# Between two attentions: where GpSimd adds the second bias, and VectorE's order of maxima and rows

## The chip, the cores and the metric

The kernel runs on one core of a Trainium2 chip. The metric is device time in microseconds (us) of one execution, as a median of runs. The five engines each follow a program of their own, in order, and meet only at semaphores: TensorE (PE) multiplies, VectorE (DVE) and ScalarE (ACT) read PE's results, GpSimd (POOL) works on what lies in on-chip memory, and SyncE (SP) issues nearly all transfers.

## The reference

One decoder layer over 16 batches of 128 tokens with 128 features: self-attention with 16 heads of 8 features and a second, decayed score; then cross-attention against a context; then a mixture of 16 experts with the best 4. Each part is followed by a residual and a layer norm.

```python
x = _layernorm(x + _L0_attn_ref(x, ...), axis=-1)             # inside: (res - mu) * rsqrt(var + EPS) * ln_g + ln_b
x = _layernorm(x + _L0_xattn_ref(x, ctx_1024, ctx_1024, ...), axis=-1)   # inside: softmax(QK), @ V, @ Wo.T + bo
x = _layernorm(x + _L0_ffn_ref(x, ...), axis=-1)
```

## The kernel before

The work goes batch by batch. Both attentions are software pipelines: a **slot** is one step of such a pipeline, it has four units (one for each group of four heads), and in one slot the stages of several batches run at once. First attention uses slots 1 to 20 (`unit1`, `slot1`, in which `bb.back(k)` is the batch k slots behind), second attention uses slots 0 to 19 of its own (`unit2`, `slot2`). Slots 17 to 20 of the first and 0 to 3 of the second run together. This stretch, called **the change-over** below, is where first attention's last rows are finished while second attention starts. Second attention's slot n is called slot n from here on, and a batch number stands in brackets.

What the first attention leaves for a batch b in the change-over, in this order: PE turns the divided values (`turn_out`, L866) and multiplies by the output weights (`out_product`, L870); DVE adds the residual (`add_residual`, L1586), takes statistics (`res_stats`, L1592) and mean and variance (`mean_var(b, 0)`, L1580); POOL takes the inverse root (`inverse_root(b, 0)`, L557 to L564); ACT centres the rows (`centre_rows`, L1267); POOL applies the gain and adds x again (`gain_and_sum`, L569 and L573); DVE takes statistics of that (`res2_stats`, L1596) and `mean_var(b, 1)`; POOL takes `inverse_root(b, 1)`; and ACT writes the row of x1 (`norm_x1`, L1272), counted by the semaphore `x1_out`. PE then turns four batches of x1 at once (`turn_x1`, L1001).

Second attention of a batch: PE projects (`project2`, L751 and L752); ACT takes the projection and its high part (`high`, L1216), POOL the remainder (`remainder`, L498), ACT the middle part (`middle`, L1220), POOL the lowest part (`lowest`, L504). SP writes the parts to DRAM (`spill`, L365 to L373) and reads them back in another layout (`stack2`, L396). `high` of batch b waits for the spill of batch b-2. PE computes scores (`score2`, L799), DVE takes each head's maximum (`maximum2`, L1529), PE turns the 16 maxima of a batch (`turn_top`, L812), ACT copies them (`take_top`, L1245), PE computes the scores again the other way round with the maximum subtracted (`score_t`, L821 and L828), ACT takes the exponent (L1236), and PE weighs the values (`weigh`, L844). `maximum2` for groups 0 and 1 of batch n runs in units 2 and 3 of slot n, for groups 2 and 3 in units 0 and 1 of slot n+1; `turn_top` of batch n is in unit 2 of slot n+1, behind all four.

POOL's `residual_bias(lo, hi)` (L641) adds the output bias `bo2` to four batches of x1 and counts `xb2`. The sums are read by DVE's `residual` of second attention (L1560), for batch n-4 in unit 3 of slot n. POOL's `power` (L578), the inverse root of second attention, comes first in POOL's slot, and DVE's `norm_out` (L1566) waits for it in unit 1.

The order on each engine is the order of its program text; no scheduler changes it. POOL and DVE run slots 5 to 12 of second attention as a loop of two passes with four slots each; PE has them written out and ACT has a loop of its own.

Of the kernel before, what the change touches and what calls it, by code (L numbers as in the profile page):

```python
# [20 lines left out]
NB = 16  # L21
# [56 lines left out]
def slot_batch(n):  # L78

    return Batch2(n // 4, n % 4)  # L80
# [13 lines left out]
def build(nc, k, out):  # L94
    with ExitStack() as ctx:
# [3 lines left out]
        def sem(name):  # L99
            return ctx.enter_context(nc.semaphore(name))  # L100
# [186 lines left out]
        xb2 = sem("xb2")  # L287
# [193 lines left out]
        def _(pool):  # L481
# [156 lines left out]
            def residual_bias(lo, hi):  # L638

                pool.wait_ge(x1_out, hi)  # L640
                pool.tensor_tensor(xb_all[:, lo:hi, :], x1[:, lo:hi, :],  # L641
                                   bo2.unsqueeze(1).broadcast_to([128, hi - lo, D]), ALU.add).then_inc(xb2, 1)
# [11 lines left out]
            def slot2(b):  # L654
                if b.back(5).live:
                    power(L2, b.back(5), 0, 4, 1, TAIL2)
                if b.back(-3).live:
                    remainder(L2, b.back(-3))
                if b.back(1).live:
                    values2(b.back(1))  # L660
                if b.back(-3).live:
                    lowest(L2, b.back(-3))

            def last_slot1(n, parts):

                b = Batch(n // 2, n % 2)
                if b.back(5).live:
                    gain_and_sum(b.back(5))
                if b.back(4).live:
                    inverse_root(b.back(4), 0)  # L670
                if parts is not None:
                    remainder(L2, parts)
                if b.back(1).live:
                    mix_values(b.back(1))
                if b.back(5).live:
                    inverse_root(b.back(5), 1)
                if parts is not None:
                    lowest(L2, parts)
# [2 lines left out]
            for n in range(14, 17):  # L681
                last_slot1(n, Batch2(0, n - 14))
            last_slot1(17, Batch2(0, 3))
            residual_bias(0, 4)
            last_slot1(18, None)
            slot2(slot_batch(1))
            residual_bias(4, 8)
            last_slot1(19, None)
            slot2(slot_batch(2))
            residual_bias(8, 12)  # L690
            last_slot1(20, None)
            slot2(slot_batch(3))
            residual_bias(12, NB)
            slot2(slot_batch(4))
            with pool.Fori(1, 3) as q:
                for i4 in range(1, 5):
                    slot2(Batch2(q, 0).back(-i4))
            for n in range(13, NB + 4):
                slot2(slot_batch(n))

            def weight(c, kk):
                u = c * KC + kk
# [751 lines left out]
        def _(dve):  # L1454
# [206 lines left out]
            def slot2(bb):  # L1661
                for g in range(NG):
                    unit2(bb, g)
# [26 lines left out]
                        values(n - 13)  # L1690
            for n in range(NB + 1, NB + 5):
                for g in range(NG):
                    unit1(n // 2, n % 2, g)
                    unit2(slot_batch(n - NB - 1), g)

            done = [0]

# [52 lines left out]
                rstep(dve.tensor_copy(r[dst][:, :, 0:sh], r[src][:, :, 0:sh]))  # L1750
                rstep(dve.tensor_tensor(r[dst][:, :, sh:NE], r[src][:, :, sh:NE], r[src][:, :, 0:NE - sh], ALU.add))

            dve.wait_ge(xb2, 1)
            slot2(slot_batch(4))
            dve.wait_ge(xb2, 4)
            with dve.Fori(1, 3) as q:
                for i4 in range(1, 5):
                    slot2(Batch2(q, 0).back(-i4))
            for n in range(13, NB + 3):
                slot2(slot_batch(n))  # L1760
            divide(L2, slot_batch(NB - 1))
            norm_out(L2, slot_batch(NB - 2), 0, res[:], x2, TAIL2, NB - 1)
# [152 lines left out]
```

## Time and profile before

| what | value |
|---|---|
| median of 3 runs | 356.65 us (356.54 to 357.73) |
| profiled execution | 357.19 us, its span 355.4 us |
| PE busy | 326.9 us (92% of the span) |
| DVE busy | 250.7 us (71%) |
| POOL busy | 215.4 us (61%) |
| ACT busy | 190.7 us (54%) |
| mean DMA rate | 152 GB/s |

The span is the time from the first to the last record on the chip; 1.8 us of the profiled execution lie around it. A row of the timeline gives start, length, engine, line, operation, what is written and read, and in brackets the idle time of the engine before it with what ended it. Starts of neighbouring rows are closer together than their lengths, since an instruction's record overlaps that of the one ahead by a little; the distance of two starts is what an instruction costs its engine.

### The profile page before, as it was taken

The numbers are of one execution on the slowest core, as the hardware profiler recorded it, in microseconds if no ns is written. First come the engines' busy times: TensorE is split into PE (matmuls) and PEld (weight loads), VectorE is DVE, ScalarE is ACT, GpSimd is POOL, SyncE is SP. The second block draws the span as 40 slices with busy tenths as digits, with TensorE's granted clock in tenths as the row PEclk, the third lists the DMA queues.
The fourth block names the chain that finished last, engine by engine and source line by source line (L and its number), as shares of the span: only waits on it lengthen the run. The fifth ranks groups of instructions, "written<-read, shape, count | busy, mean of one in ns | idle before, by whom it ended". The sixth has DMA issues, their size and how long they took to land.

```text
span 355.4 us, 11656 instructions
## 1 busy us (share of the span) xinstructions
PE 326.9 (92%) x3728; PEld 259.1 (73%) x3728; DVE 250.7 (71%) x1220; ACT 190.7 (54%) x458; POOL 215.4 (61%) x402
## 2 busy tenths in 40 slices
PE   6989899998999999975799999998889999999993
PEld 3877788887888888864588887887646765666662
DVE  1688899988989999966367767769754279254454
ACT  3586566766676665575677767754643342222220
POOL 8375899998889977788733343311134445554552
PEclk9999999999999999999999999999999999999998
DMA  7669797775677688545454544641055300624310
GB/s 219 191 188 307 233 268 229 231 223 166 202 201 208 179 235 236 168 130 140 115 133 115 145 116 99 164 106 46 10 175 183 87 32 7 180 88 144 122 32 30
DMA packets 67808, 54.07 MB, mean 152 GB/s; under 512 B 29617, under 2 KB 57649, under 8 KB 67633
## 3 DMA queue, kind: packets, MB, share of 16 engines
q1 hardware_dynamic: 67328, 52.43, 51.9%
q10 hardware_dynamic: 432, 1.05, 0.9%
q8 instruction: 25, 0.41, 0.5%
q14 instruction: 23, 0.18, 0.2%
HBM read 33.40 MB, written 20.05 MB: 150 GB/s over the span
## 4 chain that ended last, share of the span: by engine, by line
PE 45%; POOL 16%; issue 11%; DVE 9%; DMA 9%; ACT 4%; SPq 4%; POOLq 0%; ACTq 0%; DVEq 0%
PE bank L844 6%; PE bank L1109 5%; DMA parts_dram<-parts 4%; PE bank L1113 4%; PE bank L784 4%; PE bank L1122 4%; DMA stk<-parts_dram 2%; PE bank L773 2%; POOL rstd L562 2%; PE bank L799 2%; POOL rest L498 2%; DMA sup_w<-in_sup_w_dram 2%; PE bank L828 2%; PE bank L821 2%; PE bank L787 2%
## 5 line engine op out<-in xcount | busy, mean ns | idle before, releaser
L707 POOL TENSOR_TENSOR stk<-stk 128x512 f32<-128x512 f32 x32 | 40.8, 1274 | 38.3 <-ACT stk L1434 35.4
L1227 ACT ACTIVATE prob_t<-bank 128x512 f32<-128x512 f32 x64 | 38.7, 605 | 41.6 <-PE bank L787 41.6
L1518 DVE CUSTOM_DVE_ANT_0 sums<-bank,decayed_e 128x128 f32<-128x128 f32 x256 | 59.1, 287 | 0.7
L1529 DVE TENSOR_REDUCE top<-bank 128x4 bf16<-128x512 f32 x64 | 43.9, 687 | 17.2 <-PE bank L799 16.9
L1236 ACT ACTIVATE prob_t<-bank 128x512 f32<-128x512 f32 x64 | 38.8, 606 | 26.7 <-PE bank L828 26.3
L1774 DVE TENSOR_TENSOR stk<-bank,stk 128x512 f32<-128x512 f32 x32 | 22.0, 691 | 39.2 <-POOL stk L707 38.0
L1434 ACT ACTIVATE stk<-bank 128x512 f32<-128x512 f32 x32 | 19.1, 597 | 53.6 <-PE bank L1109 53.6
L1506 DVE TENSOR_TENSOR decayed_e<-bank,decay 128x512 f32<-128x512 f32 x64 | 44.0, 687 | 2.5 <-issue 1.9
L498 POOL TENSOR_TENSOR rest<-pf,parts 128x256 f32<-128x256 f32 (+1 forms) x31 | 28.1, 908 | 28.9 <-ACT parts L1216 28.8
L844 PE MATMUL bank<-prob_t,vmix 128*32 128x128 f32 x1024 | 42.6, 278 | 2.2 <-ACT pvs L1253 2.2
L784 PE MATMUL bank<-ident,sums 128*128 128x128 f32 x256 | 39.3, 276 | 2.7 <-ACT prob_t L1227 1.2
L504 POOL TENSOR_TENSOR parts<-rest,parts 128x256 bf16<-128x256 f32 (+1 forms) x31 | 28.2, 908 | 20.5 <-ACT parts L1220 20.5
L1122 PEld LDWEIGHTS bank<-w,stk 128*128 128x128 f32 x192 | 25.1, 191 | 11.9 <-issue 8.4
L1109 PE MATMUL bank<-x_t,w 128*128 128x512 f32 x64 | 32.9, 595 | 0.0
L1113 PE MATMUL bank<-x_t,w 128*128 128x512 f32 x64 | 32.7, 592 | 0.0
L844 PEld LDWEIGHTS bank<-prob_t,vmix 128*32 128x32 f32 x1024 | 25.7, 109 | 9.4 <-issue 3.9
L784 PEld LDWEIGHTS bank<-ident,sums 128*128 128x128 f32 x256 | 28.0, 141 | 5.8 <-DVE shift L1518 3.5
L763 PE MATMUL bank<-stk 128*128 128x128 bf16 x256 | 24.8, 219 | 1.2 <-DMA stk<-parts_dram 1.2
L1122 PE MATMUL bank<-w,stk 128*128 128x128 f32 x192 | 25.4, 275 | 0.0
L799 PE MATMUL bank<-stk 128*128 128x128 bf16 x256 | 24.9, 220 | 0.4 <-DVE top L1529 0.4
L773 PE MATMUL bank<-stk 128*128 128x128 bf16 x256 | 25.0, 220 | 0.0
L821 PE MATMUL bank<-stk 128*128 128x128 bf16 x256 | 24.8, 219 | 0.0
(171 smaller groups left out, 756.6 us busy)
## 6 DMA issues: line engine op xcount, KB each, us to landing
stk<-parts_dram SPq DMA_DIRECT2D x32, 384.0 KB, 4.3
stk<-shares_dram SPq DMA_DIRECT2D x64, 128.0 KB, 2.9
parts_dram<-parts SPq DMA_DIRECT2D x32, 192.0 KB, 3.5
parts_dram<-parts SPq DMA_DIRECT2D x48, 128.0 KB, 3.1
stk<-parts_dram SPq DMA_DIRECT2D x32, 192.0 KB, 2.9
parts_dram<-parts SPq DMA_DIRECT2D x32, 96.0 KB, 2.3
parts_dram<-parts SPq DMA_DIRECT2D x48, 64.0 KB, 2.1
w<-in_w_dram SPq DMA_DIRECT2D x3, 512.0 KB, 5.6
```

What stands on the lines that cost most here:

```text
L498: pool.tensor_tensor(rest[:, :, L.kinds, :], pf[:, :, L.kinds, :], by_part[b.par][:, HIGH, L.kinds, :], ALU.subtract).then_inc(L.rest, 1)
L707: pool.tensor_tensor(h1[kk % 2], sg[kk % 2], share[kk], ALU.mult).then_inc(weighted, 1)
L784: pe.matmul(bank[3][:, 128 * j:128 * j + 128], sums[g % 2][:, j, :], ident[:], start=(j == 0), stop=True, is_transpose=True, skip_group_ch ...
L844: w = pe.matmul(bank[4][32 * j:32 * j + 32, 128 * m:128 * m + 128], vmix[b.par][:, head(2 * m, j) // 2, e:e + 2, :].rearrange("p e f -> p ...
L1109: pe.matmul(bank[kk % 2][:], w1[:, 128 * kk:128 * kk + 128], xt, start=True, stop=True).then_inc(gate_mm, 1)
L1113: pe.matmul(bank[UP_BANK[u % 3]][:], w3[:, 128 * kk:128 * kk + 128], xt, start=True, stop=True).then_inc(up_mm, 1)
L1122: m = pe.matmul(bank[4 + c % 2][:, 128 * t:128 * t + 128], actt[u % 3][:, 128 * t:128 * t + 128], w2[:, kk, :], start=(kk == 0 and t == 0) ...
L1227: act.activation(prob_t[g][:].rearrange("p h t -> p (h t)"), bank[3][:], ACT.Exp).then_inc(L1.exped, 1)
L1236: act.activation(prob_t[g][:].rearrange("p h t -> p (h t)"), bank[2 + g % 2][:], ACT.Exp).then_inc(L2.exped, 1)
L1506: dve.tensor_tensor(decayed_e[:, g % 2], bank[E_BANK[g % 2]][:].rearrange("p (h t) -> p h t", h=GH), decay[:].unsqueeze(1).broadcast_to([1 ...
L1518: m = dve.tensor_tensor_reduce(out=sums[g % 2][:, j, :], in0=bank[g % 2][:, 128 * j:128 * j + 128], in1=decayed_e[:, g % 2, j, :], scale=1 ...
L1529: dve.tensor_reduce(top[:, b.par, GH * g:GH * g + GH], bank[S2_BANK[g % 2]][:].rearrange("p (h t) -> p h t", h=GH), AX.X, ALU.max).then_in ...
```

## The change

Two places of the program between the attentions are edited. POOL adds the second bias later: the four calls of `residual_bias`, which stood after slots 17, 18 (and slot 1), 19 (and slot 2) and 20 (and slot 3), now stand behind slots 3, 5, 7 and 9. DVE takes second attention's unit ahead of first attention's unit in the change-over. The loops of POOL and DVE over slots 5 to 12 are written out, and DVE waits for `xb2` in four steps (1, 2, 3, 4 ahead of slots 4, 8, 12 and 16) instead of two (1 ahead of slot 4 and 4 ahead of slot 5). PE, ACT and SP have the same program as before.

```diff
@@ POOL
             last_slot1(17, Batch2(0, 3))
-            residual_bias(0, 4)
-            last_slot1(18, None)
-            slot2(slot_batch(1))
-            residual_bias(4, 8)
-            last_slot1(19, None)
-            slot2(slot_batch(2))
-            residual_bias(8, 12)
-            last_slot1(20, None)
-            slot2(slot_batch(3))
-            residual_bias(12, NB)
-            slot2(slot_batch(4))
-            with pool.Fori(1, 3) as q:
-                for i4 in range(1, 5):
-                    slot2(Batch2(q, 0).back(-i4))
-            for n in range(13, NB + 4):
+            for n in range(1, NB + 4):
+                if n < 4:
+                    last_slot1(NB + 1 + n, None)
                 slot2(slot_batch(n))
+                if n % 2 == 1 and 3 <= n < 11:
+                    residual_bias(2 * n - 6, 2 * n - 2)
@@ DVE
             for n in range(NB + 1, NB + 5):
                 for g in range(NG):
+                    unit2(slot_batch(n - NB - 1), g)
                     unit1(n // 2, n % 2, g)
-                    unit2(slot_batch(n - NB - 1), g)
@@ DVE
-            dve.wait_ge(xb2, 1)
-            slot2(slot_batch(4))
-            dve.wait_ge(xb2, 4)
-            with dve.Fori(1, 3) as q:
-                for i4 in range(1, 5):
-                    slot2(Batch2(q, 0).back(-i4))
-            for n in range(13, NB + 3):
+            for n in range(4, NB + 3):
+                if n % 4 == 0:
+                    dve.wait_ge(xb2, n // 4)
                 slot2(slot_batch(n))
```

On DVE, slot 1 before, from the residual of batch 14 to mean and variance of batch 13's second sum (`top` is written by `maximum2`, `res10` and `res21` are the first sum of batch 14 and the second sum of batch 13, `waiter` is a filler ahead of `BN_AGGR`):

```order
L1586 TENSOR_TENSOR res10<-bank7,xb_all 128x128 [waits centre,o_out1]
L1592 BN_STATS stats<-res10 128x6 [waits tail1]
L1529 TENSOR_REDUCE top<-bank0 128x4 [waits scores2]
L1457 MEMSET waiter 128x1 [waits root0,tail1]
L1580 BN_AGGR mv<-stats 128x2
L1596 BN_STATS stats<-res21 128x6 [waits summed]
L1529 TENSOR_REDUCE top<-bank5 128x4 [waits scores2]
L1601 RECIPROCAL rden<-bank7 128x16 [waits o_tok1]
L1608 TENSOR_TENSOR attn_o<-bank7,rden 128x128 [waits o_t1,norm_step1]
L1457 MEMSET waiter 128x1 [waits root1,sum_stats]
L1580 BN_AGGR mv<-stats 128x2
L1529 TENSOR_REDUCE top<-bank0 128x4 [waits scores2]
```

The same slot on DVE now (its lines have moved up by ten, so L1519 is what L1529 was):

```order
L1519 TENSOR_REDUCE top<-bank0 128x4 [waits scores2]
L1576 TENSOR_TENSOR res10<-bank7,xb_all 128x128 [waits centre,o_out1]
L1582 BN_STATS stats<-res10 128x6 [waits tail1]
L1519 TENSOR_REDUCE top<-bank5 128x4 [waits scores2]
L1447 MEMSET waiter 128x1 [waits root0,tail1]
L1570 BN_AGGR mv<-stats 128x2
L1586 BN_STATS stats<-res21 128x6 [waits summed]
L1519 TENSOR_REDUCE top<-bank0 128x4 [waits scores2]
L1591 RECIPROCAL rden<-bank7 128x16 [waits o_tok1]
L1598 TENSOR_TENSOR attn_o<-bank7,rden 128x128 [waits o_t1,norm_step1]
L1447 MEMSET waiter 128x1 [waits root1,sum_stats]
L1570 BN_AGGR mv<-stats 128x2
```

Each maximum moved ahead of the first attention's rows of its unit: the second maximum no longer stands behind the wait for `summed`, and each `BN_AGGR` stands behind one more maximum, with its wait for `scores2`.

On POOL, slot 2 before, from the lowest part of batch 4 to the second inverse root of batch 14:

```order
L504 TENSOR_TENSOR parts0<-rest,parts0 128x2x128 [waits mid2]
L641 TENSOR_TENSOR xb_all<-x_tok,rows 128x512 [waits x1_out]
L569 TENSOR_TENSOR gained<-centred,rows 128x128 [waits centre]
L573 TENSOR_TENSOR res20<-gained,xl_all 128x128 [waits x1_out,gain]
L557 TENSOR_TENSOR veps<-mv,eps_col 128x1 [waits centre,tail1]
```

POOL now, from the remainder of batch 8 in slot 5 to that of batch 9 in slot 6:

```order
L498 TENSOR_TENSOR rest<-pf,parts0 128x2x128 [waits low2,high2]
L650 COPY vmix0<-v2_all 128x8x2x8 [waits pv2]
L504 TENSOR_TENSOR parts0<-rest,parts0 128x2x128 [waits mid2]
L641 TENSOR_TENSOR xb_all<-x_tok,rows 128x512 [waits x1_out]
L578 TENSOR_TENSOR rstd<-veps,minus_half 128x1 [waits tail2]
L498 TENSOR_TENSOR rest<-pf,parts1 128x2x128 [waits low2,high2]
```

L641 left the change-over, where it stood ahead of `gain_and_sum`, and stands ahead of `power` (L578) of the next slot.

## Rows read from the trace of the kernel before

**Rows 1.** Busy time by stretch: stretch, length, busy PE, PEld, DVE, ACT, POOL, then clock

```profile
158.00:164.00 6.00, 3.96 (x44) 3.29 (x43) 4.60 (x16) 2.53 (x9) 5.08 (x14) 1.00 0.54 136
...
183.00:189.00 6.00, 5.96 (x102) 4.79 (x92) 4.41 (x15) 4.25 (x13) 2.08 (x4) 1.00 0.52 134
```

**Rows 2.** Timeline of PE in the change-over

```profile
161.16 0.22 PE L812 MATMUL bank<-ident_bf,top 128*16 128x128 bf16 x1 [1.21 <-DVE top L1529]
...
167.98 0.22 PE L812 MATMUL bank<-ident_bf,top 128*16 128x128 bf16 x1 [2.24 <-DVE top L1529]
...
174.35 0.22 PE L812 MATMUL bank<-ident_bf,top 128*16 128x128 bf16 x1 [1.42 <-DVE top L1529]
...
177.23 0.66 PE L1001 MATMUL bank<-ident,x_tok 128*128 128x128 f32 x4 [0.92 <-ACT x_tok L1272]
```

**Rows 3.** Timeline of POOL in the change-over

```profile
157.98 1.27 POOL L641 TENSOR_TENSOR xb_all<-x_tok,rows 128x512 f32<-128x512 f32 x1
159.20 0.46 POOL L569 TENSOR_TENSOR gained<-centred,rows 128x128 f32<-128x128 f32 x1
...
160.15 0.19 POOL L557 TENSOR_TENSOR veps<-mv,eps_col 128x1 f32<-128x1 f32 x1
...
161.78 0.19 POOL L557 TENSOR_TENSOR veps<-mv,eps_col 128x1 f32<-128x1 f32 x1 [0.40 <-DVE mv L1580]
...
166.01 0.46 POOL L569 TENSOR_TENSOR gained<-centred,rows 128x128 f32<-128x128 f32 x1
...
172.38 0.46 POOL L569 TENSOR_TENSOR gained<-centred,rows 128x128 f32<-128x128 f32 x1
...
174.48 0.19 POOL L557 TENSOR_TENSOR veps<-mv,eps_col 128x1 f32<-128x1 f32 x1 [1.10 <-DVE mv L1580]
...
175.67 0.67 POOL L498 TENSOR_TENSOR rest<-pf,parts 128x256 f32<-128x256 f32 x1
...
177.49 1.27 POOL L641 TENSOR_TENSOR xb_all<-x_tok,rows 128x512 f32<-128x512 f32 x1
```

**Rows 4.** Timeline of DVE in the change-over

```profile
155.20 0.29 DVE L1608 TENSOR_TENSOR attn_o<-bank,rden 128x128 f32<-128x128 f32 x1
...
158.06 0.29 DVE L1586 TENSOR_TENSOR res<-bank,xb_all 128x128 f32<-128x128 f32 x1 [0.72 <-PE bank L870]
158.39 0.29 DVE L1592 BATCH_NORM_STATS2 stats<-res 128x6 f32<-128x128 f32 x1
158.73 0.69 DVE L1529 TENSOR_REDUCE top<-bank 128x4 bf16<-128x512 f32 x1
159.35 0.18 DVE L1580 BATCH_NORM_AGGREGATE mv<-stats 128x2 f32<-128x6 f32 x1
...
160.23 0.29 DVE L1596 BATCH_NORM_STATS2 stats<-res 128x6 f32<-128x128 f32 x1 [0.70 <-POOL res L573]
160.44 0.67 DVE L1529 TENSOR_REDUCE top<-bank 128x4 bf16<-128x512 f32 x1
...
178.66 0.69 DVE L1529 TENSOR_REDUCE top<-bank 128x4 bf16<-128x512 f32 x1 [3.03 <-PE bank L799]
```

**Rows 5.** Timeline of POOL in second attention, slot 6

```profile
190.03 0.55 POOL L578 TENSOR_TENSOR rstd<-veps,minus_half 128x1 f32<-128x1 f32 x1
192.57 0.67 POOL L498 TENSOR_TENSOR rest<-pf,parts 128x256 f32<-128x256 f32 x1 [1.99 <-ACT parts L1216]
```

**Rows 6.** Timeline of DVE in second attention, slots 6 and 7

```profile
191.76 0.34 DVE L1566 TENSOR_SCALAR c_tok<-res,mv,rstd 128x128 f32 x1
...
197.49 0.34 DVE L1566 TENSOR_SCALAR c_tok<-res,mv,rstd 128x128 f32 x1
```

**Rows 7.** Timeline of SP, late in second attention: issues of transfers

```profile
211.58 1.49 SPq L373 DMA_DIRECT2D parts_dram<-parts  x1
...
218.31 0.37 SPq L373 DMA_DIRECT2D parts_dram<-parts  x1
```

**Rows 8.** Timeline of ACT, the same place

```profile
220.83 0.40 ACT L1216 CAST parts<-pf 128x256 bf16<-128x256 f32 x1
```

## The prediction, made before the changed kernel ran

> **What bounds the kernel now.** I read the busy time by stretch first. In second attention PE works without a gap (5.96 of 6 us), with POOL at 2.08. In the change-over it is the other way round: PE is busy for 3.96 us and POOL for 5.08 [rows 1]. So the change-over is the place where time can be had, and its owner has to be found. The waits of PE name the end of the queue: for 1.21, 2.24 and 1.42 us it stands ahead of turning the maxima, for 0.92 us ahead of turning the last rows of x1 [rows 2]. But DVE's maximum is only the last link: at 160.23 DVE had itself stood 0.70 us for POOL's second sum (`summed`), and the maximum at 160.44 came right behind [rows 4]. POOL's timeline closes the argument: from `gain_and_sum` of one batch to that of the next it takes 6.81 us (159.20 to 166.01) and 6.37 us (166.01 to 172.38), and only 0.40 us of the first round is a wait of POOL's own ahead of an inverse root [rows 3]. POOL is the bound from about 157 to 176 us. Its chain ends in the remainder at 175.67, ACT's middle part, x1's last row, and PE's turning of it at 177.23, that is 1.56 after the remainder begins [rows 2, 3]. From there on PE sets the pace.
>
> **What the pieces cost.** By the distances of starts on POOL: the addition of the bias 1.22 (157.98 to 159.20), gain and sum 0.95 (159.20 to 160.15), an inverse root 1.19 (174.48 to 175.67), remainder, copy and lowest part with the short wait for ACT's middle part in them 1.82 (175.67 to 177.49) [rows 3]. The sum is complete 1.0 after gain and sum begin. On DVE: a maximum 0.62 (158.73 to 159.35), the residual 0.33 (158.06 to 158.39), its statistics ahead of a maximum 0.21 (160.23 to 160.44) [rows 4]. From the start of the maximum at 160.44 to POOL's inverse root at 161.78, through reciprocal, normalising and mean and variance, 1.34 [rows 3, 4]. From the start of mean and variance to POOL's start I take 0.25: its length of 0.18 [rows 4] and an estimate of 0.07 for the signal.
>
> **Part one, the bias later.** Three additions leave POOL's chain ahead of the last `inverse_root`: -3.66 if nothing else comes late. The fourth (177.49) was behind the chain.
>
> **Part two, the maxima first.** This takes the second maximum of each batch from behind the wait for `summed`, but puts a maximum and its wait for PE's scores ahead of each thing that POOL waits for. I follow it date by date.
>
> Unit 2 of slot 0: normalising of batch 14 (155.20 [rows 4]) now stands behind a maximum: 0.62, and about 0.2 until its scores are there. By PE's timeline its other work covers 0.5 of these 0.8, so 0.3 reach PE, and as much reaches POOL. `gain_and_sum` of batch 13 starts at 159.20 - 1.22 + 0.31 = 158.29.
>
> Slot 1: PE runs 0.28 later, so the maximum that began at 158.73 begins at 159.01. Residual at 159.62, statistics at 159.95, second maximum at 160.16, mean and variance of batch 14 at 160.77 instead of 159.35 [rows 4]. POOL, which would be ready at 158.29 + 0.95 = 159.24, starts that inverse root at 161.02 and could start the next at 162.21. But the third maximum begins at 160.77 + 0.11 + 0.21 = 161.09, and by the 1.34 above POOL's next root starts at 162.43 (before: 161.78 [rows 3]). From there 1.19 + 1.82: `gain_and_sum` of batch 14 at 165.45, 0.56 earlier than before.
>
> Slot 2: POOL is ready for the next root at 166.40 and DVE delivers at 166.63, since its maxima of this slot wait for PE no longer. 166.63 + 1.19 + 1.19 + 1.82 = 170.83 for `gain_and_sum` of batch 15, 1.55 earlier than 172.38. PE turns the second batch's maxima at about 166.5 instead of 167.98.
>
> Slot 3: the sum is ready at 171.83, DVE takes statistics, one maximum (0.62, where before the same length stood there) and mean and variance. POOL's root is at 172.93 instead of 174.48, the remainder at 174.12, and PE turns x1 1.56 later, at 175.68 instead of 177.23. PE's waits for maxima are gone (the third batch's are there by 171.4), but it now stands for x1 from about 174.3 on, since POOL's chain is still last. **The change-over gets shorter by 1.55 us:** 3.66 gained, 2.11 given back by the new order on DVE.
>
> **Where the bias goes.** Behind slot 3 the first addition runs from 177.49 - 1.55 = 175.94 to 177.21. DVE waits for it ahead of slot 4, whose first maximum would start at 178.66 - 1.55 = 177.11 [rows 3, 4]: about 0.15 late. Queued behind it are that maximum and the first division of second attention; PE needs these 0.2 us and more after. I count zero. The other three stand in slots 5, 7 and 9, each ahead of `power`. That would move from 190.03 to 191.25 in slot 6 of before, and end at 191.80; DVE's `norm_out` begins at 191.76 [rows 5, 6]. So it comes 0.1 late, DVE's next maximum waits for PE anyway, and POOL has 1.99 us of idle time to absorb 1.22 [rows 5]. Zero again; without that cover it would be 1.2 each. The waits ahead of slots 8, 12 and 16 are met slots before.
>
> **Loops written out.** Dynamic instructions and two backward branches go away on DVE and POOL in a stretch where PE is never late for them: zero, bounded by 0.1 us per loop either way. The page "Runtime: NRT & Kernel Launch" of the Trainium skill, section "Instruction fetch mechanics", says that a taken branch out of the fetched window stalls the engine for a fetch, which would make writing out a gain of its own. The rows show POOL waiting for ACT in these slots [rows 5], so what it would save lies beside PE either way.
>
> **What may take it back.** SP's chain in second attention (read back, write the next parts, wait for landing) took 6.73 us for one slot (211.58 to 218.31 [rows 7]) where DVE, driven by PE, takes 5.73 (191.76 to 197.49 [rows 6]), so it falls behind. Late in the stretch ACT's high part (220.83) starts just when the spill issued at 218.31 has landed, 2.5 us later [rows 7, 8]; PE's next product is 0.6 us behind that. The slack is used up. SP's chain is fed by POOL's lowest parts, which come 1.55 earlier from slot 3 on, but it follows only by 1.3 to 1.5, as it was limited by its own issues. I take 0.15 off. And single issues of SP last about a microsecond longer than others (1.49 against 0.37 [rows 7]), so one more or one fewer of these moves the end by up to 1 us.
>
> **Sum.** -1.55 + 0.15 = -1.4. On the profiled execution that is 357.19 - 1.4 = 355.8, with the span at 354.0. That execution lies 0.54 above the median; on the median 356.65 - 1.4 = **355.25 us**.
>
> **Rivals.**
> - The transfers take most of it: one more long issue of SP, or its chain not following, and ACT's high parts of batches 13 to 15 wait up to 1 us. Gain 0.4: 356.25. For it speaks that the slack there is nil; against, that such long issues were in the trace before too. Chance 0.2.
> - DVE's order costs less than I worked out, because PE's scores come earlier or my 2.11 counts waits twice. At the far end all of 3.66 stays: 353.0; halfway 2.6: 354.05. PE's three waits for maxima add up to 4.87 us [rows 2], which allows it. Against it: the late mean and variance of batch 14. Chance 0.25 for a gain above 1.8.
> - Slower: the new order on DVE costs more than the bias gave. Each unit's maximum waits for PE, PE waits for the normalised rows behind it, and POOL waits for both. I find 2.1 given back; it turns the sign at 3.7. That takes a PE later by 0.8 in each of slots 1 to 3, for example because the parts of batch 1 or 2 are not back from DRAM. At 2 us each for two slots instead of 2.11 in all it is +0.5, and with the bias of slot 3 then stopping DVE's slot 4 by 1.2 it is +1.9: 358.5. Against it: PE waited for none of these parts in the change-over; all its waits there name DVE or ACT [rows 2]. Chance 0.05.
> - Only the move of the bias matters, or it does nothing since the maxima were the bound: then PE's last wait would not be for x1, but the trace has that wait. It gives 356.65. In the 0.2 above.
>
> **How the numbers follow.** Forecast (gain 0.9 to 1.8) 0.5, transfers 0.2, larger gain 0.25, slower 0.05. The range holds 8 in 10 from 354.1 to 356.6. A measurement of this kernel tells about 0.5%, or 1.78 us, from no change. Faster by more than that takes a time under 354.87: the larger gain and a little of the forecast's edge, 0.29. Within 0.5%: 0.66. Slower: 0.05.
>
> **What would show it.** POOL's `gain_and_sum` at about 158.3, 165.4 and 170.8 in the changed trace, and waits of POOL ahead of inverse roots in slot 1 (1.8 us) that were not there. PE's turning of maxima no longer stands for 2.24 us. PE's wait for x1 remains, 1.3 us. L641 four times between 176 and 212 with PE going on without a gap. It is wrong if PE waits for x1 no longer, if ACT's high parts start after a spill's landing by more than 0.5 us, or if the gain is already gone at PE's turning of x1.

## The result, and the profile after

The changed kernel took 358.91 us in the median of 20 runs (355.81 to 360.95), the kernel before 356.80 us (20 runs, 355.68 to 360.16), so the medians lie 2.1 us apart. The ratio, which goes by the means (358.91 and 357.23), is 1.0047 with a 95% interval of 1.0025 to 1.0069: slower by 0.47%, 1.7 us, which is just inside the 0.5% that I had set as what a measurement can tell, while the interval leaves out 1. The forecast was 355.25 us with a range up to 356.6, so the sign and the range were both missed.

The profiled execution of the changed kernel took 360.95 us, its span 359.1. It is the longest of its 20 and lies 2.0 above their median, where that of before lies 0.4 above its own. So its trace shows which losses can occur, with more time lost than in most of its executions; its granted clock over the whole span, 0.989, is the mean of the 20, though. By its dates, as starts against those of before: the change-over begins (POOL's gain for batch 12) at 153.74 against 153.41, PE turns the last rows of x1 at 178.33 against 177.23 [rows 2], and the routing shares of the experts' part are ready at 258.19 against 254.45. The change-over, forecast 1.55 shorter, is 0.77 longer (24.59 against 23.82), and second attention behind it is 2.64 longer (79.86 against 77.22). With the 0.33 ahead of both that is the difference of the spans, 3.7.

Busy time by stretch of the changed kernel (stretch, its length, then busy us and instructions of PE, PE's weight loads, DVE, ACT and POOL, granted clock, DMA share, GB/s); these answer to [rows 1]:

```profile
158.00:164.00 6.00, 3.31 (x23) 2.58 (x24) 3.30 (x12) 2.03 (x7) 2.85 (x10) 0.66 0.50 131
164.00:170.00 6.00, 5.82 (x62) 5.15 (x61) 3.45 (x12) 3.82 (x11) 3.94 (x11) 0.77 0.53 133
200.00:220.00 20.00, 18.59 (x294) 15.16 (x297) 13.60 (x38) 13.01 (x36) 9.20 (x16) 1.00 0.51 129
```

And the kernel before, in the last of these stretches:

```profile
200.00:220.00 20.00, 19.87 (x326) 16.59 (x322) 14.49 (x45) 13.49 (x37) 7.42 (x14) 1.00 0.51 124
```

In the first stretch every engine does less than before; nothing is the bound there in the sense of a full engine. PE's granted clock, 1.00 in these stretches before, is 0.66 and 0.77 now: a part of them ran at the lower level of 1.2 GHz. And in second attention PE has gaps (18.59 of 20 us), where before had next to none (19.87).

PE's timeline in slot 1, to be read against [rows 2]:

```profile
158.18 0.49 PE L860 MATMUL bank<-late_w,attn_ot 128*128 128x128 f32 x2 [0.92 <-ACT x_t L1355]
158.95 0.39 PE L789 MATMUL bank<-stk 128*128 128x128 bf16 x4
160.41 0.66 PE L847 MATMUL bank<-ident,pvs 128*128 128x128 f32 x2 [1.07 <-DVE res L1576]
162.28 0.28 PE L802 MATMUL bank<-ident_bf,top 128*16 128x128 bf16 x1 [0.36 <-DVE top L1519]
163.64 0.47 PE L856 MATMUL bank<-ident,attn_o 128*128 128x128 f32 x1 [1.08 <-DVE attn_o L1598]
163.91 0.63 PE L789 MATMUL bank<-stk 128*128 128x128 bf16 x4
178.33 0.66 PE L991 MATMUL bank<-ident,x_tok 128*128 128x128 f32 x4 [1.32 <-ACT x_tok L1262]
```

The waits for maxima went down as intended: 0.36 here where 1.21 stood. But there is a wait that before did not have: L847 is `to_tokens` of batch 15, and it stands 1.07 us for DVE's residual of batch 14. Four score products of a unit took 0.39 at 158.95 and take 0.63 at 163.91: that is the clock. The wait for x1 at the end is there, 1.32, as forecast.

DVE in the same slot:

```profile
159.38 0.69 DVE L1519 TENSOR_REDUCE top<-bank 128x4 bf16<-128x512 f32 x1 [1.39 <-PE bank L789]
159.98 0.28 DVE L1576 TENSOR_TENSOR res<-bank,xb_all 128x128 f32<-128x128 f32 x1
161.53 0.69 DVE L1519 TENSOR_REDUCE top<-bank 128x4 bf16<-128x512 f32 x1 [0.94 <-PE bank L789]
162.15 0.18 DVE L1570 BATCH_NORM_AGGREGATE mv<-stats 128x2 f32<-128x6 f32 x1
```

The first maximum stands 1.39 us for PE, the residual waits behind it, PE waits for the residual, and the second maximum waits for PE. Each engine stands for the other in turn.

POOL's timeline, against [rows 3]:

```profile
158.63 0.46 POOL L569 TENSOR_TENSOR gained<-centred,rows 128x128 f32<-128x128 f32 x1
162.41 0.19 POOL L557 TENSOR_TENSOR veps<-mv,eps_col 128x1 f32<-128x1 f32 x1 [2.79 <-DVE mv L1570]
166.75 0.45 POOL L569 TENSOR_TENSOR gained<-centred,rows 128x128 f32<-128x128 f32 x1
173.38 0.45 POOL L569 TENSOR_TENSOR gained<-centred,rows 128x128 f32<-128x128 f32 x1
178.58 1.27 POOL L641 TENSOR_TENSOR xb_all<-x_tok,rows 128x512 f32<-128x512 f32 x1
```

POOL is spared 1.22 us in each slot by the additions that left, and in slot 1 it then stands 2.79 us for mean and variance (1.8 was forecast).

Second attention: the waits of PE and ACT from 178 to 257 us (what waited, for what: us in all, times, longest), and SP's issues around two late landings.

```profile
PE bank L860 <- ACT attn_ot L1251: 2.7, 4, 1.1
ACT parts L1206 <- DMA parts_dram<-parts: 2.1, 2, 1.2
```

```profile
182.54 0.37 SPq L370 DMA_DIRECT2D parts_dram<-parts  x1
183.09 0.37 SPq L373 DMA_DIRECT2D parts_dram<-parts  x1
184.89 1.27 SPq L396 DMA_DIRECT2D stk<-parts_dram  x2
186.42 0.95 SPq L365 DMA_DIRECT2D parts_dram<-parts  x2
...
188.67 0.37 SPq L373 DMA_DIRECT2D parts_dram<-parts  x1
191.97 1.26 SPq L396 DMA_DIRECT2D stk<-parts_dram  x2
...
195.80 0.37 SPq L373 DMA_DIRECT2D parts_dram<-parts  x1
199.36 1.27 SPq L396 DMA_DIRECT2D stk<-parts_dram  x2
```

SP's program is in order: it waits for a batch's spill to land, reads it back (L396), and only then writes the next batch (L365 to L373). A read-back follows the last write of its batch by 1.80 us at 184.89, and by 3.30 and 3.56 at 191.97 and 199.36. ACT's high part (L1206) waits for the spill of two batches before, the copy `attn_ot` (L1251) stands behind it on ACT, and PE's product (L860) waits for that.

### The profile page after: what moved, and what is told of

Same layout as the page of the kernel before. It is cut to its first block, busy times and chain, and to the rows that moved or that the text cites. A ratio compares the mean times of both kernels' runs of the same rounds, so it can differ in the third digit from the quotient of the medians.

```text
span 359.1 us, 11539 instructions
## 1 busy us (share of the span) xinstructions
PE 329.2 (92%) x3728; PEld 260.6 (73%) x3728; DVE 250.9 (70%) x1220; ACT 190.6 (53%) x458; POOL 215.0 (60%) x402
## 4 chain that ended last, share of the span: by engine, by line
PE 55%; issue 11%; DVE 10%; DMA 9%; SPq 6%; ACT 6%; POOL 2%; ACTq 0%; POOLq 0%; DVEq 0%
PE bank L834 7%; PE bank L774 6%; DMA parts_dram<-parts 5%; PE bank L1099 5%; PE bank L1103 4%; PE bank L1112 4%; PE bank L763 3%; PE bank L777 3%; PE bank L731 3%; PE bank L789 3%; DMA stk<-parts_dram 2%; PE bank L753 2%; PE bank L847 2%; PE bank L818 2%; PE bank L811 2%
## 5 line engine op out<-in xcount | busy, mean ns | idle before, releaser
L1519 DVE TENSOR_REDUCE top<-bank 128x4 bf16<-128x512 f32 x64 | 44.0, 687 | 25.1 <-PE bank L789 21.2
```

The costliest lines, as they stand in the source:

```text
L1519: dve.tensor_reduce(top[:, b.par, GH * g:GH * g + GH], bank[S2_BANK[g % 2]][:].rearrange("p (h t) -> p h t", h=GH), AX.X, ALU.max).then_in ...
```

## Experiments

All keep the full computation. "Change-over" is, in the profiled execution of each kernel, the time from POOL's gain for batch 12 to PE's turning of the last rows of x1; "behind" is from there to the routing shares; "last read-back" is SP's L396 of batch 15, and "tail" from it to the routing shares. Ratios are of means, against executions of the kernel before that belong to the same group of runs. Its median moved from group to group: 356.80 us beside after, 358.54 beside e1 to e4, 357.33 beside e6 and f1 to f3, 357.16 beside e7 and f4. So kernels of different groups are compared by their ratios, and the absolute times that the expectations of e1, e2 and e4 name, set against 356.8, are read as distances from the kernel before. A profiled execution is one of many, so a difference of a few tenths between its columns may be chance.

| kernel | median, ratio [95%] | change-over | behind | last read-back, tail |
|---|---|---|---|---|
| before | | 23.82 | 77.22 | 239.44, 15.0 |
| after | 358.91, 1.0047 [1.0025, 1.0069] | 24.59 | 79.86 | 242.35, 15.8 |
| e1_bias_only | 356.97, 0.9968 [0.9943, 0.9994] | 20.54 | 80.11 | 239.42, 15.0 |
| e2_order_only | 360.44, 1.0049 [1.0017, 1.0080] | 25.82 | 78.03 | 241.75, 15.3 |
| e3_loops_only | 357.57, 0.9978 [0.9949, 1.0007] | 23.80 | 78.66 | 240.29, 15.5 |
| e4_residual_first | 358.21, 0.9999 [0.9969, 1.0030] | 21.75 | 79.64 | 238.33, 15.5 |
| e6_filler | 357.47, 1.0007 [0.9981, 1.0033] | 22.92 | 77.65 | 238.23, 15.8 |
| e7_four_parts_after | 357.24, 1.0007 [0.9973, 1.0042] | 22.92 | 77.65 | 238.70, 15.1 |
| f1_spill_ahead_before | 356.68, 0.9977 [0.9950, 1.0004] | 23.76 | 77.55 | 231.13, 22.8 |
| f2_spill_ahead_after | 357.39, 0.9999 [0.9975, 1.0023] | 23.63 | 77.60 | 231.56, 23.2 |
| f3_spill_ahead_bias | 353.76, 0.9901 [0.9877, 0.9924] | 20.53 | 77.65 | 227.38, 23.2 |
| f4_spill_ahead_sum_last | 353.59, 0.9898 [0.9854, 0.9942] | 20.04 | 77.32 | 228.65, 23.2 |

My theory after the two traces had three parts: DVE's new order costs more than the late bias gives (the missed wait), PE's clock falls in the gaps that it opens, and SP's chain takes what is left. The rivals: the bias additions or the written-out loops do harm in second attention, or the clock alone is the loss.

### The parts one by one

**Bias and loops, without the new order on DVE (e1).**

```diff
 DVE, from the changed kernel
                 for g in range(NG):
-                    unit2(slot_batch(n - NB - 1), g)
                     unit1(n // 2, n % 2, g)
+                    unit2(slot_batch(n - NB - 1), g)
```

> The changed kernel with VectorE's old order in the change-over (first attention's unit ahead of second attention's): the bias moved and the loops written out, and nothing else. Theory A (the new order on VectorE is what costs): to_tokens of batch 15 waits for the residual of batch 14, which now stands behind a maximum, PE idles and falls to its lower clock, and the transfers of second attention start later against PE. Then this kernel has no such wait, PE turns the last rows of x1 about 3 us earlier than before (near 174 instead of 177.2), and the time is 353.8 to 354.8 us, 2 to 3 below before. Theory B (the bias costs where it now stands, in slots 3, 5, 7 and 9, ahead of the inverse root of second attention): the time stays near 358.9. Theory C (written out loops cost): near 358.9 too.

**The order alone, on the kernel before (e2):** the same two lines the other way round, nothing else.

> The kernel before with VectorE's new order in the change-over, and nothing else. Theory A: POOL stands 2.8, 1.5 and 1.2 us ahead of its inverse roots in the changed kernel; the additions of the bias (1.22 us each) would fit in these waits, so this kernel takes about what the changed one takes, 358.3 to 359.5 us, and shows the lower clock near 160 us. Theories B and C: 356.8 us or less.

**The loops alone (e3).**

```diff
 DVE, from the kernel before (POOL likewise, up to NB + 4)
-            with dve.Fori(1, 3) as q:
-                for i4 in range(1, 5):
-                    slot2(Batch2(q, 0).back(-i4))
-            for n in range(13, NB + 3):
+            for n in range(5, NB + 3):
```

> The kernel before with the loops of POOL and VectorE over slots 5 to 12 written out, and nothing else. Theories A and B: 356.8 us, within 0.3. Theory C: near 358.9.

The new order is the part that costs. e1, which is the change without it, is faster than before (0.9968, 1.1 us where 2 to 3 were expected) with a change-over of 20.54; e2, which is it alone, is slower (1.0049) with 25.82. Moving the bias out therefore is worth 3.28 us of the change-over, against 3.66 forecast: the first batch of it brings the whole 1.22, the next only 0.81, because POOL then stands 0.64 us for mean and variance of batch 14 in slot 1:

```profile
160.00 0.19 POOL L557 TENSOR_TENSOR veps<-mv,eps_col 128x1 f32<-128x1 f32 x1 [0.64 <-DVE mv L1570]
```

The loops show no difference that can be measured (0.9978, the interval holds 1). The rule of the Trainium skill, page "Runtime: NRT & Kernel Launch", section "Instruction fetch mechanics", that a taken branch can stall an engine, would have made them a gain; no run here shows one, and a gain of up to 0.5% isn't excluded by this one either.

e1 leaves a question of its own: 3.3 us less in the change-over, but only about 1.1 us at the end, and 80.11 behind the change-over where 77.22 stood. Its last read-back comes at 239.42, before had it at 239.44. The waits of e1 in second attention:

```profile
PE bank L860 <- ACT attn_ot L1251: 3.1, 4, 1.4
ACT parts L1206 <- DMA parts_dram<-parts: 2.4, 3, 1.2
```

### The missed wait

**The residual back ahead of the first maximum (e4).** The changed kernel, with that one instruction in its old place ahead of the maximum of unit 0.

```diff
 DVE
                 for g in range(NG):
+                    bb = Batch(n // 2, n % 2)
+                    if g == 0 and bb.back(4).live:
+                        add_residual(bb.back(4))
                     unit2(slot_batch(n - NB - 1), g)
-                    unit1(n // 2, n % 2, g)
+                    unit1(n // 2, n % 2, g, False)
```

With `False`, `unit1` leaves out its own `add_residual`.

> The changed kernel with one instruction of a slot put back: add_residual stands ahead of the maximum of unit 0, all else is as in the changed kernel. Theory A: to_tokens of batch 15 no longer waits 1.07 us, PE's clock stays at its upper level, the change-over is about 2.2 us shorter than in the changed kernel, PE turns the last rows of x1 near 176, and the time is 356 to 356.7. If the clock falls all the same, 357.5 to 358. Theories B and C: 358.9.

PE no longer waits for the residual, POOL's wait ahead of the root of batch 14 is 1.42 instead of 2.79, the clock is 1.00, and the change-over goes from 24.59 to 21.75. Part of that is the clock, which e6 and e7 below take apart: against their 22.92, at a clock of 1.00 as well, the place of this one instruction is worth 1.17. The rest of the order costs another 1.21 (21.75 against 20.54 of e1); which of its rows does is not taken apart. PE and POOL in slot 1 of e4:

```profile
157.86 0.39 PE L847 MATMUL bank<-ident,pvs 128*128 128x128 f32 x2
159.73 0.19 POOL L557 TENSOR_TENSOR veps<-mv,eps_col 128x1 f32<-128x1 f32 x1 [1.42 <-DVE mv L1570]
```

The ratio at the end is 0.9999, no gain that can be measured, and behind the change-over it needs 79.64, nearly what e1 did.

### The clock

**Products without use in PE's gaps (e6).** The changed kernel with 3, 4 and 4 products of zeros into a free bank, at the end of slot 0 and ahead of units 1 and 3 of slot 1, so that PE has work in its waits.

```diff
 PE
+                    if (n, g) == (NB + 2, 1):
+                        filler(4)
+                    if (n, g) == (NB + 2, 3):
+                        filler(4)
                     unit1(Batch(n // 2, n % 2), g)
 ...
                 if n == NB + 1:
+                    pe.wait_ge(L1.exped, NG * NB)
+                    filler(3)
                     pe.wait_ge(turn1_ev, 2)
```

> The changed kernel with PE kept at work in the waits of slot 1: three, four and four extra products of zeros (128x512, bf16) into a bank that nobody reads then, at the end of slot 0 and ahead of units 1 and 3 of slot 1. If the low clock between 158 and 167 us cost what its durations say (about 1.2 us), PE turns the last rows of x1 1.0 to 1.4 us sooner after the start of the change-over than in the changed kernel, with a clock of 1.00 there. If the clock was only a sign of idle time and cost nothing, that distance stays as it is (24.6 us from the first gained to x1's last turning). The whole time moves by less than that, 0 to 1.2 us under the changed kernel, since the transfers hold second attention.

The clock stayed at 1.00 in 158 to 164 us, and the change-over is 22.92, that is 1.67 less than in the trace of after (1.0 to 1.4 was expected). That would look like a proof that fillers hold the clock, but e7, below, has the same order and no fillers, and its trace shows 1.00 as well, with the same 22.92:

```profile
158.00:164.00 6.00, 3.06 (x31) 2.40 (x30) 3.99 (x13) 2.09 (x7) 3.13 (x12) 1.00 0.53 131
```

PE is busy for only 3.06 us there, less than in after's trace. So the fall doesn't occur in every execution. By the difference to e7 it costs about 1.7 us in the trace of after, and 0.7 in f2, where it came one stretch later (1.00, then 0.72 from 164 to 170).

How often it occurs no trace can tell, but the record has the mean granted clock over the whole span for every execution. Its mean is 0.989 for after (20 executions), 0.985 for e2 (12), 0.990 for e7 (10) and 0.990 for f2 (12), all with the new order; 0.992 for before (35, 29 and 13 executions), 0.994 for e1 (12) and 0.995 for f3 (6) with the old one; and 0.994 for e6 (10), which has the new order and the fillers. e7's profiled execution, at 0.997, is the highest of its ten, which go down to 0.983 in the longest of them. So the trace without the fall is probably the uncommon one, and the fillers probably do hold the clock. That isn't shown, since the number covers the whole span, and the traces show falls at its start and end too (0.57 from 8 to 12 us in e1 and e3, 0.50 from 352 us on in before). A faster kernel the fillers didn't make: e6 took 1.0007 and e7, without them, 1.0007.

### The chain of transfers

**Four buffers of parts (e7).** The changed kernel, with second attention's parts in four buffers instead of two, on ACT, POOL and SP, so that ACT's high part waits for the spill of four batches before and no longer of two.

```diff
 ACT, the wait of high
-                if not isinstance(b.n, int) or b.n >= 2:
+                if L is L2:
+                    if not isinstance(b.n, int) or b.n >= 4:
+                        act.wait_ge(L.spilled[b.par], b.pair * L.spill_step - L.spill_step)
+                elif not isinstance(b.n, int) or b.n >= 2:
                     act.wait_ge(L.spilled[b.par], b.pair * L.spill_step)
```

> The changed kernel with four buffers for the parts in second attention instead of two (the halves that only first attention uses), so that ScalarE's high part of batch b waits for the spill of batch b-4 and no longer of b-2; SP's order is untouched. If PE's waits in second attention come through ScalarE's wait for a landing, they go, and from x1's last turning to the routing shares it takes 77.2 to 78.2 us instead of 79.9. If the chain of transfers also holds the scores directly (reading back too late for score2), a part of it stays, 78.5 to 79.9, with waits of PE's scores for the read back parts. The change-over stays as in the changed kernel (24.6 us) or 1.2 to 1.7 shorter where the clock does not fall.

ACT doesn't wait for landings any more, the second attention takes 77.65, and the median is 1.0007 of before: about 0.4% less than after's 1.0047, at intervals that overlap a little. The trace alone proves less than it seems to: e6, with the same order, the same change-over of 22.92 and ACT's wait still in place (0.4 us in all), takes 77.65 as well.

Over all traces the waits say it better. PE's waits for `attn_ot` at the output product, and ACT's for a landing, from 178 to 257 us, add up to 3.1 and 2.4 us in e1 (80.11 behind the change-over), 2.7 and 2.1 in after (79.86) and e4 (79.64), 1.6 and 1.2 in e3 (78.66), 0.9 and 0.8 in e2 (78.03). In e6 they are 0.5 and 0.4, and in before, e7 and f1 to f4 the view lists none; there the time behind is 77.22 to 77.65. So the time above 77.6 is PE's wait less 0.4 to 0.7 us in each of the six that have one: the loss behind the change-over comes to PE this way.

**The spill ahead of the read-back (f1 to f3).** SP now writes batch b+1 (`b.back(-1)`) before it waits for the landing of batch b and reads it back, so that this landing lies beside the issues of the next write. f1 is that on the kernel before, f2 on the changed kernel, f3 on e1.

```diff
 SP, second attention from batch 4 on
+            def quad2_ahead(q):
+                for i4 in range(4):
+                    b = Batch2(q, i4)
+                    if b.back(-1).live:
+                        spill(L2, b.back(-1))
+                    stack2(b)
 ...
             with sp.Fori(1, 3) as q:
-                quad2(q)
-            quad2(3)
+                quad2_ahead(q)
+            quad2_ahead(3)
```

> The kernel before with one pair of steps of SP exchanged from batch 4 of second attention on: the parts of batch b+1 are written out ahead of reading batch b back, so that reading back no longer stands right behind the wait for its own parts to land. Nothing else. Theory D (the chain of transfers, 6.3 us a round against PE's 5.73, is what second attention waits for late): 0.2 to 1.0 us under the kernel before, and none of ScalarE's high parts waits for a landing. Rival (second attention is bound by PE, and the chain only runs beside it): no difference, ratio 0.999 to 1.001.

> The changed kernel with the same exchange on SP. Theory D: second attention takes 77.2 us from x1's last turning to the routing shares as in the profile of before, instead of 79.9, and what is left against the kernel before is the longer change-over: 0 to 0.8 us slower, ratio 1.000 to 1.002. Rival (the loss in second attention is the bias where it now stands, or the loops): 79.9 stays, and the ratio stays near 1.005.

> The bias later and the loops written out, VectorE's order as before, and the same exchange on SP. Theory D: the 3.3 us that the change-over gets shorter reach the end: ratio 0.990 to 0.993, 2.5 to 3.6 us under the kernel before, where the same kernel without the exchange had 0.9968. Rival: no better than 0.9968.

SP's issues in f3: the read-back at 177.22 now follows the last write of the next batch (176.66), and its own batch had landed long before.

```profile
170.61 0.37 SPq L373 DMA_DIRECT2D parts_dram<-parts  x1
171.33 1.27 SPq L396 DMA_DIRECT2D stk<-parts_dram  x2
173.44 0.96 SPq L365 DMA_DIRECT2D parts_dram<-parts  x2
174.94 0.38 SPq L369 DMA_DIRECT2D parts_dram<-parts  x1
175.51 0.97 SPq L370 DMA_DIRECT2D parts_dram<-parts  x1
176.66 0.37 SPq L373 DMA_DIRECT2D parts_dram<-parts  x1
177.22 1.24 SPq L396 DMA_DIRECT2D stk<-parts_dram  x2
```

And the busy time of f3 in second attention, where PE is without a gap:

```profile
200.00:220.00 20.00, 19.83 (x312) 16.20 (x309) 14.84 (x43) 14.22 (x40) 8.37 (x15) 1.00 0.61 149
220.00:237.00 17.00, 17.00 (x268) 14.81 (x266) 12.00 (x39) 10.51 (x27) 4.39 (x9) 1.00 0.47 119
```

The last column of the table says the rest. In every kernel with the old order on SP the routing shares come 15.0 to 15.8 us after the last read-back, whatever the change-over took. That alone doesn't make the chain the bound: before, e6 and e7 are in that list and need no more behind the change-over (77.22 to 77.65) than the kernels with the exchange, so there PE's own work ends about when the chain lets it. But a change-over shorter than theirs finds the chain in its way: e1's, 2.4 to 3.3 us shorter, ends second attention at about the same time after its start, 100.65 us against 100.57 (e6, e7) and 101.04 (before). With the exchange the tail is 22.8 to 23.2, so the chain is some 7.5 us ahead of its use, and the time behind the change-over is 77.55 to 77.65 for all of f1, f2 and f3, so f3, with e1's change-over, ends it after 98.18. On e1 the exchange alone turns 0.9968 [0.9943, 0.9994] into 0.9901 [0.9877, 0.9924]; on the kernel before it shows nothing for sure (0.9977, interval up to 1.0004). It lets the gain of the change-over through rather than being one.

f2 and f3 ran on one chip and differ in DVE's order alone: 357.39 against 353.76. The order costs 3.6 us where nothing hides it, 3.1 of them in the change-over of the traces (23.63 against 20.53).

### One more order on DVE

**Only the second sum's statistics behind the maximum (f4).** f3, but in unit 1 the maximum goes ahead of `res2_stats`, the one instruction that had waited for POOL in [rows 4].

```diff
 DVE, from f3
                 for g in range(NG):
-                    unit1(n // 2, n % 2, g)
+                    unit1(n // 2, n % 2, g, False)
                     unit2(slot_batch(n - NB - 1), g)
+                    bb = Batch(n // 2, n % 2)
+                    if g == 1 and bb.back(5).live:
+                        res2_stats(bb.back(5))
```

Here `False` makes `unit1` leave out its own `res2_stats`.

> The bias later, SP's exchange, and on VectorE the old order with one difference: the maximum of unit 1 stands ahead of the statistics of the second sum alone (the one instruction that waits for POOL's sum), all other rows of first attention ahead of the maxima as before. If the wait for the sum is what held the maxima, PE turns them sooner (third batch 0.3 to 1 us), but POOL's chain is what ends last, so the change-over stays at 20.5 us within 0.3 and the ratio at 0.990 as without this step. If maxima ahead are worth something by themselves: under 0.988.

353.59 against 353.76 for f3, 0.9898 against 0.9901 with intervals of 0.2 to 0.4% either side: no difference shown. Its change-over is 20.04 against 20.53 in one trace each. f3 and f4 both beat before, by 1%, and by their ratios after by 1.5%.

## Why the prediction was wrong, point by point

The traces lie 5.1 us from the forecast (3.7 longer instead of 1.4 shorter), in two parts of about the same size: the change-over is 2.32 longer than forecast (+0.77 instead of -1.55), and second attention 2.49 (+2.64 instead of +0.15). The rest is the 0.33 ahead of both. So two terms of the sum failed, and the headings below take them in the order of the prediction.

**What bounds the kernel: right.** POOL's chain was the bound of the change-over. Taking the additions out of it shortened the stretch by 3.28 (e1). PE's wait for x1 is still there too, 1.32 us for 1.3 forecast.

**Part one, the bias, -3.66: nearly right,** by 0.4 too much, for POOL's wait for mean and variance in slot 1.

**Part two, 2.11 given back by the order: the first step that failed.** The dates, each moved to a common start of the change-over (0.33 off for after, 0.16 on for e7, whose clock did not fall):

| | forecast | e7, clock 1.00 | after, clock 0.66 |
|---|---|---|---|
| gain of batch 13 | 158.29 | 158.30 | 158.30 |
| first maximum of slot 1 | 159.01 | 159.04 | 159.05 |
| residual of batch 14 | 159.62 | 159.65 | 159.65 |
| second maximum | 160.16 | 160.75 | 161.20 |
| inverse root of batch 14 | 161.02 | 161.62 | 162.08 |
| gain of batch 14 | 165.45 | 165.97 | 166.42 |
| gain of batch 15 | 170.83 | 171.38 | 173.05 |
| last inverse root | 172.93 | 173.59 | 175.25 |
| PE turns x1 | 175.68 | 176.33 | 178.00 |

Up to the residual the forecast holds to 0.04 us. Then the second maximum, which I put 0.21 behind the statistics, comes 0.6 later: it needs PE's scores, and PE was standing for the residual. In e7, by the same order without the fall:

```profile
159.49 0.28 DVE L1582 TENSOR_TENSOR res<-bank,xb_all 128x128 f32<-128x128 f32 x1
159.92 0.41 PE L850 MATMUL bank<-ident,pvs 128*128 128x128 f32 x2 [1.07 <-DVE res L1582]
160.16 0.61 PE L792 MATMUL bank<-stk 128*128 128x128 bf16 x8
160.59 0.69 DVE L1525 TENSOR_REDUCE top<-bank 128x4 bf16<-128x512 f32 x1 [0.49 <-PE bank L792]
```

The wait is `pe.wait_ge(L.tail, b.n * steps - steps + 1)` in `to_tokens` (L853 of before): PE may write columns 256 to 511 of bank 7 for batch 15 only when DVE's residual has read columns 128 to 255 of it for batch 14. The two don't share a value, only the bank. I had listed what POOL waits for behind each maximum, and not what PE does. These 0.6 run through to the end and are the whole miss of the unslowed trace (0.65). (Set against e1, the same 0.65 is 0.38 less from the bias and 2.38 instead of 2.11 for the order.) The second term had no place in the sum at all: PE's clock. In after's trace, set against e7's, its fall adds 1.67 (178.00 against 176.33), and turns a change-over that is 0.90 shorter into one that is 0.77 longer. Against the same kernel with the old order (e1, 20.54) the order costs 2.38 without the fall and 4.05 with it.

**Where the bias goes: right.** The first addition does stop DVE's first maximum of slot 4, which starts 1.55 us behind PE's turning of x1 (179.88) where before it was 1.43: 0.12 for 0.15 forecast. The additions stand at 178.58, 191.11, 202.79 and 214.43. POOL's rows at the second one, against [rows 5], show `power` right behind it and no trouble for the remainder, which still waits for ACT:

```profile
191.11 1.27 POOL L641 TENSOR_TENSOR xb_all<-x_tok,rows 128x512 f32<-128x512 f32 x1
192.34 0.55 POOL L578 TENSOR_TENSOR rstd<-veps,minus_half 128x1 f32<-128x1 f32 x1
193.65 0.67 POOL L498 TENSOR_TENSOR rest<-pf,parts 128x256 f32<-128x256 f32 x1 [0.75 <-ACT parts L1206]
```

f3 has them too, and PE has no gap there. **Loops: zero, as far as e3 can tell.** No run shows the bound of 0.1 us per loop; e3's interval reaches from -0.5% to +0.1%.

**What may take it back, 0.15: the second step that failed.** The place was right: the slack is used up, and ACT's high part goes when a spill lands. The size was not. I read that SP's chain would follow by 1.3 to 1.5 of an earlier start. In e1 POOL's lowest part of slot 2 came 1.7 earlier (168.87 against 170.53; 2.05 with a common start of the change-over) and the chain's last read-back 0.02 earlier (0.41). It doesn't follow, since it is bound by its own issues and landings: SP wrote that part only from 172.42 on, as it stood till 170.90 for the landing of the batch before. In after the chain was also fed late: SP stood 1.5 us for PE ahead of the read-back at 170.49 and 1.6 us for POOL's parts, and its last read-back is 2.58 later than before's by the start of the change-over (88.61 us behind it against 86.03). In all, in after's trace second attention takes 2.64 back, in e1 2.89, in e4 2.42. This was the rival "the transfers take most of it", with a chance of 0.2; I had priced it at one late transfer, 1 us, and there were several.

**The slower rival: the mechanism, at 0.05.** "The new order on DVE costs more than the bias gave" is what happened, but not from a batch back late from DRAM. It turned the sign at 3.7; the order costs 2.4 to 4.1 in the traces and the chain keeps most of what is left, so the point was lower than I put it. That the two rivals don't exclude each other, one loss in the change-over and one behind it, was left out of the chances.

**What stays open.** In how many executions of the changed kernel the clock falls in the change-over, and so how the 2.1 us of the medians divide between order, clock and chain: e6, meant to hold the clock, and e7, which frees ACT from the chain, both come to 1.0007, and f2 to 0.9999, with intervals of 0.25 to 0.35% either side. And why it is 1.8 us from the last write to the read-back at one time and 3.3 to 4.1 at another.

## What to carry to other kernels

Before an instruction is moved on an in-order engine, list every wait on it, on all engines, also those that only guard a shared buffer: the wait that lengthened this change-over first was for a shared bank, not for data. If a stretch gets shorter, look for a chain in the next stretch that runs on its own time, here write, landing, read-back; what it doesn't follow is lost, and issuing the next write ahead of the wait for a landing can free it. A gain that vanishes at the end may be worth keeping until its next bound is found: the late bias gave 0.3% alone and 1% with the exchange on SP.

## What the runs showed of the hardware

**The clock.** PE's granted clock fell from 1.00 to 0.66 in 158 to 164 us of after (0.67 in e2), with PE idle for 0.92 and 1.07 us ahead of L860 and L847 in between short groups, and stayed at 1.00 in e7 with the same gaps and less busy time (3.06 us of 6). Two kernels whose change-over has the old order fell as well: e3 to 0.81 and f1 to 0.78 in the same stretch, with change-overs of 23.80 and 23.76 against 23.82 of before at 1.00. So the same instructions can meet either level, and in these traces the fall cost nothing where POOL's chain was the bound and about 1.7 us in after, where POOL and DVE stood for PE.

**Landings and issues.** From the last write of a batch (L373) to its read-back it was 1.75 to 1.80 us in 7 of 12 rounds of second attention both before and after, but 3.30 and 3.56 in after, and 4.11 in e1 (166.79 to 170.90):

```profile
166.79 0.48 SPq L373 DMA_DIRECT2D parts_dram<-parts  x1
170.90 1.25 SPq L396 DMA_DIRECT2D stk<-parts_dram  x2
```

The page "DMA: Bandwidth & Descriptors" of the Trainium skill, section "Latency and other measured facts", gives an access to HBM as 0.2 us on average and 2 us at high load, as the main part of a transfer's fixed cost. A spread of that size is what the rows show, 2.3 us between the shortest and the longest; no run here ties a late landing to the core's own load: its DMA share between the last write and the landing was 0.31 and 0.30 in the two late cases of after and 0.35 in e1's, against 0.44 and 0.60 in two ordinary ones (183.09 and 203.16 of after). And single issues of SP that last 0.37 us as a rule lasted 1.3 to 2.2 now and then in every trace, at other places in each.
